# New turns for four woven chains, other fillers on TensorE, and a warm-up run in the set-up of a two-layer decoder

## The reference

```python
x = x + attn_low_rank(norm(x))        # 16 heads of 16, k and v by a rank-64 factor, rotated by head
x = x + attn_over_heads(norm(x), ctx) # 16 heads of 64; softmax over heads within a token
x = x + routed_ffn(norm(x))           # the 128 best of 256 tokens, 256 -> 1024 -> 256, gelu
x = x + sparse_attn(norm(x))          # 16 heads; keeps the largest scores of a row, zeros elsewhere
x = x + masked_attn(norm(x), ctx)     # 16 heads of 16; keys past the valid length masked
x = x + ternary_linear(norm(x))       # weights quantized to -1, 0, 1
```

## Time and profile before

| | |
|---|---|
| timed runs, median (lowest to highest) | 5739.61 us (5729.64 to 5741.0), 3 runs |
| profiled execution | 5731.2 us, its span 5729.4 us |
| granted TensorE clock, mean | 0.976 |
| TensorE busy | 5178.4 us, 90% |
| VectorE busy | 4514.2 us, 79% |
| ScalarE busy | 3732.4 us, 65% |
| GpSimd busy | 2281.7 us, 40% |
| chain that ended last, by engine | TensorE 55%, VectorE 23%, ScalarE 12%, GpSimd 4%, issue 3% |

### The profile page before, as it was taken

How to read it: one execution, slowest core, us unless ns; L and a number is a source line. 1 busy time by engine, 2 the same in 40 slices (tenths; PEclk the granted TensorE clock), 3 DMA queues, 4 the chain that set the end, 5 groups by cost and what they waited for, 6 DMA issues and landing times.

```text
span 5729.4 us, 115571 instructions
## 1 busy us (share of the span) xinstructions
PE 5178.4 (90%) x40598; PEld 3679.5 (64%) x40598; DVE 4514.2 (79%) x16125; ACT 3732.4 (65%) x9377; POOL 2281.7 (40%) x4100
## 2 busy tenths in 40 slices
PE   6899999998999999999999899999999999999876
PEld 4666666666666666666666666666666666666653
DVE  2577898778897788888888788877889778897774
ACT  3665677666676666667666676766677666676642
POOL 0233444334443344444344444333444334443432
PEclk7999999999999999999999999999999999999986
DMA  2000000000000000000000000000000000000000
GB/s 93 6 5 5 9 9 9 8 5 5 9 9 9 8 5 7 7 9 9 9 5 8 6 9 9 9 5 7 7 9 9 9 5 7 9 7 9 5 1 6
DMA packets 29351, 53.13 MB, mean 9 GB/s; under 512 B 8145, under 2 KB 9810, under 8 KB 27986
## 3 DMA queue, kind: packets, MB, share of 16 engines
q1 hardware_dynamic: 28770, 45.73, 2.5%
HBM read 37.33 MB, written 8.39 MB: 8 GB/s over the span
## 4 chain that ended last, share of the span: by engine, by line
PE 55%; DVE 23%; ACT 12%; POOL 4%; issue 3%; DVEq 0%; POOLq 0%; ACTq 0%
PE bankH L745 9%; DVE m_nm L512 6%; PE bankM L559 6%; DVE wk L1080 6%; PE bankH L785 4%; DVE m L1076 4%; PE bankM L588 3%; PE bankT L486 3%; PE bankT L603 3%; PE bankM L502 2%; PE bankM L555 2%; PE bankT L464 2%; PE bankT L472 2%; PE bankH L768 2%; PE bankM L472 2%
## 5 line engine op out<-in xcount | busy, mean ns | idle before, releaser
L512 DVE TENSOR_REDUCE m_nm<-bankM 128x2 f32<-128x512 f32 x1024 | 641.4, 681 | 266.4 <-PE bankM L502 265.2
L1080 DVE MATCH_REPLACE8 wk<-m,wk 128x256 f32<-128x256 f32 x2048 | 822.0, 409 | 0.0
L1076 DVE MAX8 m<-wk 128x8 f32<-128x256 f32 x2048 | 758.3, 412 | 0.0
L1110 POOL TENSOR_TENSOR t_pr<-wk,sc 128x256 f32<-128x256 f32 x1024 | 729.9, 734 | 1.7 <-issue 0.6
L1113 POOL TENSOR_TENSOR t_pr<-t_pr,sc 128x256 f32<-128x256 f32 x1024 | 729.7, 734 | 0.0
L1101 POOL TENSOR_SCALAR mx<-m 128x2 f32<-128x2 f32 x512 | 114.6, 224 | 1327.9 <-DVE wk L1080 1323.2
L843 ACT ACTIVATE xk_area<-bankH,xb 64x256 f32<-64x256 f32 x1024 | 480.0, 469 | 174.1 <-PE bankH L745 155.9
L559 PE MATMUL bankM<-m_q,m_kT 32*128 32x512 f32 x2048 | 537.5, 603 | 0.0
L612 ACT ACTIVATE t_pt<-bankT 128x512 f32<-128x512 f32 x512 | 308.8, 603 | 296.6 <-PE bankT L603 292.1
L1037 ACT ACTIVATE t_pr<-t_pr,t_nm 128x256 f32<-128x256 f32 x1024 | 472.7, 512 | 24.9 <-POOL t_pr L1113 18.6
L1076 DVE MAX8 m<-sc 128x8 f32<-128x256 f32 x1024 | 380.4, 413 | 126.2 <-ACT sc L1027 122.7
(11 more groups left out here) (224 smaller groups left out, 11715.3 us busy)
## 6 DMA issues: line engine op xcount, KB each, us to landing
xin<-x_in SPq DMA_DIRECT2D x32, 256.0 KB, 2.6
ctxA<-ctx_in SPq DMA_DIRECT2D x32, 256.0 KB, 2.6
ctxB<-ctx_in SPq DMA_DIRECT2D x32, 256.0 KB, 2.6
out<-x SPq DMA_DIRECT2D x32, 256.0 KB, 2.0
w<-w_w SPq DMA_DIRECT2D x2, 1024.0 KB
xwq<-w_xwq SPq DMA_DIRECT2D x1, 1024.0 KB
xwk<-w_xwk SPq DMA_DIRECT2D x1, 1024.0 KB
xwv<-w_xwv SPq DMA_DIRECT2D x1, 1024.0 KB
```

Source lines behind the costliest of these rows:

```text
L512: nc.vector.tensor_reduce(b["nm"][:, t, 4 * e + k, :], bankM[k][:].rearrange("p (j s) -> p j s", j=2), AX.X, ALU.max, negate=True).then_in ...
L1076: link.inc(nc.vector.max(top, src[:, t, :]))
L1080: m = nc.vector.match_replace(out=wk[:, k, t, :], in_to_replace=take, in_values=src[:, t, :], imm_value=-BIG)
L1110: nc.gpsimd.tensor_tensor(taken[:, u % 2, t, :], wk[:, u % 2, t, :], sc[:, u % 3, t, :], ALU.subtract).then_inc(g["sp_tk"], 1)
```

## The change

- ORDER, ORDER_FIRST and ORDER_LAST are written anew for all four engines. The number of turns per chain stays, but for one more turn per batch of c and of m on TensorE.
- The tables of fillers are written anew. Chains c and m get three more places each in tensor_at: ahead of the pair scores 4 and 12 (behind the wait for the maxima), and behind the last scores, in a turn of its own, behind a wait for maximum 13.
- In the loop (four laps) the fillers are 117 before (t 41, h 55, c 12, m 9) and 96 after (t 31, h 35, c 4, m 26); ahead of it 44 and 66, behind it 171 and 190. In all 1034 and 928.
- The set-up pass gets 19 fillers more (FILL_START), made of the constant ones, since the weights of the others are not loaded yet.
- In the first block TensorE runs 48 fillers of the same kind.

Lines of the diff (of the orders two lines; the rest of these tables is left out):

```diff
@@ -62,89 +62,93 @@
 ORDER = {
     "pe": runs("""
-        h c h2 t c t h t c h2 t c t h c h2 c h t h2 c h c h3 c t h c t2 c h t c3 h c3 t c2 m h c4 t c2 t c h t c m c h3 t m h2 m c h m c t m h2
...
+        c h2 t h c t h t h c h c h t c t h2 c h2 c t h2 c h2 t h2 c2 h c t2 c3 t h c3 m c3 h t c5 h c t c m h t c t c m2 t m h c2 h t m h3 t c t
...
-FILL = {"t": ["01333123", "23001010", "02110201", "03010331"],
-        "h": ["11333200000", "02333010311", "23031011220", "03200100310"],
-        "c": ["32", "32", "00", "11"],
-        "m": ["020", "202", "001", "002"]}
-FILL_FIRST = {"t": ["01331000"],
-        "h": ["33311100301", "33313000200"],
-        "m": ["023", "000"]}
-FILL_LAST = {"t": ["23904018", "51553774", "45562660"],
-        "h": ["05661340304", "03220121402"],
-        "c": ["10", "30", "53", "46"],
-        "m": ["200"]}
-CHUNKS = {"pe": dict(h=57, t=39, c=30, m=29),
+FILL = {"t": ["22310101", "20200131", "10201100", "12100120"],
+        "h": ["20321000021", "32321000001", "11030010110", "01200000100"],
+        "c": ["00110", "00000", "00000", "00110"],
+        "m": ["201020", "100032", "112233", "101001"]}
+WARM = 48
+FILL_START = {"m": ["033355"]}
+FILL_FIRST = {"t": ["20613002"],
+        "h": ["38130000100", "82612000000"],
+        "m": ["001222", "240400"]}
+FILL_LAST = {"t": ["00100612", "21440387", "32724780"],
+        "h": ["90110000000", "70690850004"],
+        "c": ["31200", "04143", "91960", "00928"],
+        "m": ["000600"]}
+CHUNKS = {"pe": dict(h=57, t=39, c=31, m=30),
@@ -316,6 +320,12 @@
 
                 sp.dma_start(xin[:], x_in[0]).then_inc(g["x_in"], 16)
 
+            @block.tensor
+            def _(pe):
+                pe.wait_ge(s_set, 1)
+                for _ in range(WARM):
+                    nc.tensor.matmul(bankT[0][:, 0:P], ones[:], ones[:], start=True, stop=True)
+
             @block.vector
             def _(dve):
                 nc.vector.memset(ones[:], 1.0).then_inc(s_set, 1)
@@ -415,9 +425,13 @@
 
         def fill(letter, place, to):
 
-            if lap["of"] == "all":
-                for _ in range(int(FILLERS[letter][lap["n"] - first[letter]][place])):
-                    nc.tensor.matmul(to, w["xwq"][:, 0, 0:P], w["xwq"][:, 1, 0:P], start=True, stop=True)
+            table = {"start": FILL_START, "all": FILLERS}[lap["of"]]
+            if letter in table:
+                for _ in range(int(table[letter][lap["n"] - first[letter]][place])):
+                    if lap["of"] == "start":
+                        nc.tensor.matmul(to, ones[:], ones[:], start=True, stop=True)
+                    else:
+                        nc.tensor.matmul(to, w["xwq"][:, 0, 0:P], w["xwq"][:, 1, 0:P], start=True, stop=True)
 
         def ln_dve(dve, k, x, ln):
             for t in range(NT):
@@ -581,7 +595,7 @@
             if i == 4:
                 pe.wait_ge(*at(g[n + "_ot"], 1))
             if i % 4 == 0:
-                fill("c" if n == "crs" else "m", i // 4 + (n == "mla"), bank[:, S:S + P])
+                fill("c" if n == "crs" else "m", 3 + i // 4 + (n == "mla"), bank[:, S:S + P])
             for x in range(2):
                 for j in range(2):
                     r = 32 * (2 * x + j)
@@ -1133,7 +1147,12 @@
                         pe.wait_ge(*at(g["lin_o"], 1))
                 if u >= 4:
                     pe.wait_ge(*at(g[n + "_nm"], u - 4 + SIDE))
+                if u in (4, 12):
+                    fill("c" if masked else "m", u // 8 + (not masked), bankM[0][:, 0:P])
                 pair_scores(n, b, range(u, u + SIDE), masked)
+            yield
+            pe.wait_ge(*at(g[n + "_nm"], 13))
+            fill("c" if masked else "m", 2 + (not masked), bankM[0][:, 0:P])
             yield from shift_rows(pe, n, b, bankM[2])
             done = 0
             for v in range(0, 2 * PAIRS, DEEP):
```

More of the change, by code:

```diff
@@ L98 @@
+        t3 h t3 c t2 h c t h2 t4 c h t2 c t h t6 h t h t h t9 c2 t6 c t33 c t3 c t3 c t6 c t c6"""),
 }
@@ new lines @@
+    "dve": runs("""
+        t h2 t c t2 c m h2 c3 m t c3 t c t c4 t c2 t c2 t c4 t5 m t5 h t3 h t2 h t2 h m t c h c2 t2 c3 t c t2 h t2 c t m3 h2 m t2 m h2 m3 t m h
+        m3 h t m2 h m2 t3 h t h t3 h t12 h2 c h t h t h5 t3 h t m3 t4 h t3 m h t h t2 h t c2 m h c2 t h c12 t c4 t8 m t4 m t5 h m c3 t2 h t2 c h
+        c h2 c t3 c h t h t4 h c t m4 h t m4 t m3 h2 m t m3 h2 m t c t2 h t4 h t h t11 h3 t h t3 h5 t8 m3 t4 h c h c2 t c h m2 h2 t h2 t2 c12 t
+        c4 t16 m t4 m t3 c2 m c h t2 c h c t c h t h c t3 h c t m3 h m t2 m3 h m h t m h m3 h t h m4 t h t2 h t h t2 h t4 h t4 c t6 h3 t h t4 h
+        t h4 t3 m3 h t3 h t c3 m c t h3 t2 h t h c12 t c4 t3 m t9 m t6 m t3 m t2 c2 h c t3 c2 h c h t c t h t3 c t h2 m4 t m2 h m h m t h m4 h t
+        m4 h t h2 t5 h2 t2 h t11 h3 t h t3 h5 t6 m2 h2 m2 t3 h t"""),
```

95 lines of the change are left out of this document (45 added, 50 removed).

## The result

The changed kernel takes 5645.94 us in the median of 3 runs (5645.81 to 5650.78), before 5739.61: a ratio of 0.9851 (95% interval 0.9831 to 0.9871). It is faster, as forecast, but by three times as much: 5708 was predicted, and the range went down to 5656 only, so the result lies 10 us outside it.

The account below looks back on a forecast made before the run. The prediction took TensorE as nearly full in the loop, the rest being the weave of four chains. Loop -19, set-up -5 and last batch -4 made -28 on 5731.2, 5703; plus 5 for the timed median, 5708 us, range 5656 to 5760.

Parts of the forecast that it names:

- Order of the loop: Loop on TensorE: more steps directly behind the one they need add up to +34 us of waits; half taken, +17.
- durations stay: Loop: the new order gives each engine other turns, but each step takes as long as before; no size given.
- Fillers of the loop: Loop on TensorE: 21 fewer fillers per period at 0.244 us each, 5.1 us per period, -36 us in seven.
- Rest of the last pass: Last pass, taken together with the first laps: more fillers and other turns, +-10 us, counted as 0.
- Set-up: Before the loop: warm-up fillers cost 0, 19 fillers in the first batch's attention raise the clock; -5 us, bounds -10 and +8.
- The rule of the Trainium skill: Set-up: TensorE loses its speed in each wait between bursts, so the set-up would cost +8 us, total 5721.
- Last batch: End of the program: context projections moved behind the last t projection, more fillers ahead of the shift; -4 us, bounds +5 and -9.
- the first (the weave closes further, 5665): Loop: the new order hides half of the 13 us of waits per period, -45 us more, about 5665; chance 0.22.
- The third, the clock that falls in the loop: Loop: fewer fillers let the clock fall, 4 us each, 14 falls, 5764 us; chance 0.14, with a worse set-up.

Follow-up runs that it names:

- e2: Changed kernel with the loop's old order on all engines and its new fillers kept: 5787.28 us, ratio 1.009.
- e3: Changed kernel with one other piece put between t's scores and the step ahead at 8 places per loop period: 5712.71 us, ratio 0.9957.
- e9: Changed kernel with the pairs split, t's scores moved earlier at 7 of 8 places and later at one: 5680.85 us, ratio 0.991.
- e6: Changed kernel with all old loop fillers (117 per period) in the new order: 5703.64 us, ratio 0.9953.
- e8: Changed kernel with the last pass's old order and old fillers: 5674.52 us, ratio 0.9898.
- e12: Changed kernel with the last pass's old fillers in its new order: 5665.09 us, ratio 0.9879.
- e7: Changed kernel with no fillers in the loop: 5664.03 us, ratio 0.9881.
- e16: Changed kernel with only c's and m's fillers in the loop and none in the set-up pass: 5664.09 us, ratio 0.9878.
- e18: Changed kernel without set-up-pass fillers, t's and h's loop fillers in the second of four laps only, 10 overlapping pairs instead of 8: 5662.42 us, ratio 0.9881.
- e14: Changed kernel with c's and m's loop fillers as before, 87 fillers per period instead of 96: 5645.31 us, ratio 0.9844.
- e15: Changed kernel with 10 fitting neighbours per period instead of 8 and no fillers in the set-up pass: 5645.23 us, ratio 0.9845.
- e4: Kernel before with t's scores moved to give 9 fitting neighbours per period instead of 3: 5742.6 us, ratio 1.0015.
- e5: Changed kernel with t's scores directly ahead of the transposed-score step instead of behind it, at 8 places per period: 5650.85 us, ratio 0.9856.

## Why the prediction was right in its direction and wrong in its size

Step by step, with the prediction's own parts:

- *Order of the loop* (+17 forecast): the step that failed. The waits of close neighbours came at their places (L637 6.0 us instead of 3.9, L772 5.5 instead of L758's 5.0), but other waits went (5 instead of 10 ahead of L617), and TensorE's idle sum stayed at 51 us per period: 0 instead of +17. And the order did a thing that I had no term for. I had counted neighbours for their waits only, and "durations stay" was wrong: 8 instead of 3 pairs of m's or c's step and t's scores per period run at the same time. With the new fillers and the clock held, the new order makes a period 675.4 us where the old one has 682.2 (e2): about -7 us per period, some -48 in seven, instead of +17. e3 and e9 put the 8 pairs at 5 to 8 us of a period.
- *Fillers of the loop* (-36 forecast): right for TensorE's busy time (5.3 us less per period, 37 in seven), wrong as a term that stands by itself. In the old order the new fillers give 1 to 2 us per period where the clock holds and cost 12 where it falls (e2); in the new order they give 7 to 11 (e6, 58 us in all). The sum added two terms that need each other. Loop and first laps together came out at -61 us where I had -19.
- *Rest of the last pass* (0 forecast, +-10): -23 from the 29th store to the last output projection. The term was left at zero since I had no count for it, and this is the second step that failed. The new order and fillers of that pass bring the last t batch forward by 24 us against the 29th store; both have a part in it (e8, e12).
- *Set-up* (-5 forecast): 0. The warm-up run cost nothing, as forecast, and gave nothing. After 5.43 us of waiting the work at 19.07 ran at half speed, with a granted clock of 0.50. The rule of the Trainium skill that I set against it (TensorE: Matmul & The Clock Gate, "HAM oscillation — how this bites in real kernels") was right for the warm-up run. The bounds for the 19 fillers, -10 and +8, were about right as bounds, since traces came out 4 us before and 8 us behind the kernel before, but the mean of the twelve lies 1.6 us behind that of the eight without, where I had taken -5 for both edits. That the large pass began at 91.69 instead of 89.09 in the trace of after is one draw of this.
- *Last batch* (-4 forecast): -4.05, from the output projection to the last store. That the figures agree this closely is luck, as the parts don't all. The clock is up for part of it, as the steps at its end show, TensorE in order of time:

```profile
5560.36 2.83 PE L486 MATMUL bankT<-swo,lnT_xT 128*128 128x256 f32 x8 [0.69 <-ACT lnT_xT L680]
5562.99 2.77 PE L478 MATMUL bankM<-ctxB,cwk 128*128 128x256 f32 x8
5565.60 1.89 PE L486 MATMUL bankM<-cwv,ctxB 128*128 128x256 f32 x8
5567.33 0.60 PE L465 MATMUL bankM<-ident,m_pT 128*128 128x128 f32 x4
...
5588.75 3.85 PE L434 MATMUL bankM<-xwq 128*128 128x128 f32 x18 [0.77 <-DVE m_nm L526]
5592.53 0.41 PE L550 MATMUL bankM<-ident_b,m_sp 128*32 128x128 bf16 x16
```

  The two context projections take 2.8 and 1.9 us, 4.7 where I had taken 5.5, the transposes behind them 0.60 instead of 1.12. They start 6.97 us behind the t projection's start, before 7.71, where I had them 1.6 us later. L550 now follows the fillers at 0.41 instead of 0.62.

The sum by the measured terms: +3 up to the large pass, -61 from there to the 29th store, -23 and -4 make -85 of the span. Of the rivals, the first (the weave closes further, 5665) came nearest, by another mechanism than its own: it asked for waits to close. The third, the clock that falls in the loop, did not happen in this kernel, but it is what e2, e7, e16 and e18 show one step away from it, at 10 to 18 us a fall and not 4.

What stays open: which wait holds the period at 675.5 when TensorE has 3 us less to do (e14, e15), why six more overlapping pairs gave the kernel before nothing (e4), and so why the new order pays with the new fillers only (e6). VectorE's larger share of the chain of waits (29% instead of 23%) points to t's top-k, but no run took that away.

## What to carry to other kernels

When an order of instructions is changed, count neighbours twice: for the waits between them, and for pairs that can run at the same time, since a pair of steps with 32-row matrices in different row groups took 1.25 us instead of 2.4. Such a pair saves time only where nothing else holds the loop (e4 and e15 gained none). An order and its fillers are one change: their terms can't be added, since each alone gave 2 us per period at most and the two together 8. Filler matmuls belong to one order: after each change of the order look at the granted clock lap by lap, and then thin the fillers out in the laps whose clock holds without them. A part for which there is no count, like the order of the last pass here, needs a wider bound than a zero with ten either way; when both traces are there, comparing when the last long chain starts shows where the gain lies.

## What the runs showed of the hardware

- Matmuls of different chains, into different PSUM banks, in float32 and bf16 mixed, overlap when they stand next to each other in TensorE's queue and use different groups of 32 rows (1.25 us for a pair), in either order (e5). With the same groups they don't (2.11 us for two neighbours of after), and one other step between them ends it (e3: none left of 8).
- A set-up pass of the same instructions took 12 us more or less from one kernel to the next: the set-up passes of e3 and e7 are the same as after's, and the first wide projections of the large pass started at 84.83 in e3, at 91.69 in after, and at 97.37 in e7. From 68 to 84 us the granted clock is 1.00 in e3 and 0.50 in e7. Without the 19 fillers the spread was under 3 us. A gain of a few microseconds in a set-up at low clock can't be read from one profiled execution.
- Whether the clock falls differs between repetitions of the same instructions within one execution (e16: 686.1, 672.4, 688.1, 670.2 us for four periods in a row, the granted clock of their first laps 0.90, 0.99, 0.88 and 1.00).
